# A decoder-block kernel on one core: every engine's order of work rewritten between the first convolution and the last picks

## The reference, cut to what matters

```python
h = _L0_tok_ref(x, positions, ...)                   # [16, 128, 64]
h = h + _L0_attn_ref(_layernorm(h), ...)             # linear recurrence over 128 steps
h = h + _L0_ffn_ref(_layernorm(h), ...)              # 8 experts, one chosen per token

# _L0_tok_ref
h = gelu(conv1d(onehot, w1, b1, 3)); h = gelu(conv1d(h, w2, b2, 2))
ctx = sigmoid(conv1d(h, w3, b3, 1))
amps = emb[ids] * ctx
for s in range(4):
    z = (position - center) / width_s
    basis_total += exp(-0.5 * z * z) * cos(phase + 2 * pi * z) * amp_scale * scale_weights[s] ** 2
field = einsum('bsp,bsd->bpd', basis_total, amps)

# _L0_attn_ref: complex poles, states h_t = A h_{t-1} + u_t, y = Re(C h)
# _L0_ffn_ref
H = gelu(xf @ W1 + b1)                               # 64 -> 256
probs = softmax(H @ Wg + bg)                         # 8 experts
out = probs[chosen] * (H @ Wd[chosen] + bd[chosen])
```

## Time and profile before

| | us |
|---|---|
| Time, median of 3 runs | 111.67 |
| Lowest and highest run | 111.58, 112.59 |
| The profiled execution's own time | 111.52 |
| Its span in the profile | 109.6 |
| TensorE busy (723 instructions) | 100.5 (92%) |
| VectorE busy (230) | 90.0 (82%) |
| ScalarE busy (126) | 70.8 (65%) |
| GpSimd busy (101) | 51.0 (47%) |
| TensorE's granted clock | 1.00 |

### The profile page before, as it was taken

One profiled execution on the slowest core, in us unless ns is written; L12 is line 12 of the kernel. 1 busy time (PEld: TensorE's weight loads), 2 busy tenths in 40 slices (PEclk: granted clock), 3 DMA queues, 4 the chain that ended last, 5 costly groups with the idle time before them and its releaser, 6 DMA issues.

```text
span 109.6 us, 2018 instructions
## 1 busy us (share of the span) xinstructions
PE 100.5 (92%) x723; PEld 64.3 (59%) x723; DVE 90.0 (82%) x230; ACT 70.8 (65%) x126; POOL 51.0 (47%) x101
## 2 busy tenths in 40 slices
PE   5979999999999978869899999999999799999970
PEld 2356785364434576347567477876696476776640
DVE  0359999999999949999999599678999956199892
ACT  4604599999999999999869438454758513551000
POOL 7798998899980007205509426256005000000670
PEclk9999999999999999999999999999999999999999
DMA  3999700000000100000000000000000000000044
GB/s 91 269 233 408 283 0 0 3 0 0 6 0 4 5 0 0 0 0 6 0 0 0 0 6 0 0 0 0 0 0 9 0 0 0 0 0 0 0 96 96
DMA packets 4313, 4.15 MB, mean 38 GB/s; under 512 B 3280, under 2 KB 3536, under 8 KB 4176
## 3 DMA queue, kind: packets, MB, share of 16 engines
q1 hardware_dynamic: 4160, 3.92, 12.5%
q10 hardware_dynamic: 144, 0.12, 0.4%
HBM read 3.50 MB, written 0.52 MB: 37 GB/s over the span
## 4 chain that ended last, share of the span: by engine, by line
PE 42%; ACT 38%; DVE 8%; DMA 4%; issue 4%; POOL 2%; ACTq 0%; DVEq 0%
PE pair L1080 14%; ACT wave L476 8%; PE bank L1042 7%; ACT bell L466 7%; ACT bell L470 5%; ACT L425 5%; DMA ids<-x 4%; DVE pair L819 3%; PE hid_pair L1053 3%; PE pair L951 3%; ACT angle L514 3%; PE pair L921 2%; ACT h L460 2%; PE hid_pair L1063 2%; ACT dist L455 2%
## 5 line engine op out<-in xcount | busy, mean ns | idle before, releaser
L379 POOL TENSOR_SCALAR var_eps<-mean_var 128x4 f32<-128x4 f32 x8 | 3.7, 458 | 33.0 <-DVE mean_var L747 33.0
L819 DVE COPY_PREDICATED pair<-later,pair 128x256 f32<-128x256 int32 (+3 forms) x30 | 12.3, 409 | 5.3 <-PE pair L1080 4.6
L921 PE MATMUL pair<-warm 128*128 128x512 bf16 x53 | 13.3, 380 | 0.0
L732 DVE SCALAR_TENSOR_TENSOR bell<-bell,scale_w,wave 128x512 f32<-128x512 f32 x16 | 10.8, 743 | 0.0
L1080 PE MATMUL pair<-wd_high,H_high 128*128 128x512 f32 x32 | 10.8, 418 | 0.0
L921 PE MATMUL hid_pair<-warm 128*128 128x512 bf16 x30 | 9.0, 455 | 1.3 <-POOL warm L298 1.3
L1080 PE MATMUL pair<-wd_low,H_high 128*128 128x512 f32 x32 | 10.0, 394 | 0.0
L395 POOL TENSOR_TENSOR angle<-picked,prob 128x256 f32<-128x256 f32 x3 | 1.8, 613 | 17.2 <-DVE prob L843 17.2
L521 ACT ACTIVATE bell<-hid_pair,sm 128x512 f32<-128x512 f32 x8 | 5.0, 680 | 7.2 <-PE hid_pair L1053 7.2
L675 DVE TENSOR_TENSOR wave<-dist,inv_width 128x2048 f32<-128x2048 f32 x4 | 9.3, 2356 | 0.0
L965 PE MATMUL pair<-h,w_sb 128*64 128x512 f32 x40 | 9.1, 597 | 0.0
(11 more groups left out here) (166 smaller groups left out, 226.1 us busy)
## 6 DMA issues: line engine op xcount, KB each, us to landing
ids<-x SPq DMA_DIRECT2D x2, 512.0 KB, 5.7
posb<-positions SPq DMA_DIRECT2D x1, 768.0 KB, 8.1
wd_sb<-wd SPq DMA_DIRECT2D x1, 512.0 KB, 9.1
out<-angle SPq DMA_DIRECT2D x3, 128.0 KB, 2.0
st_sb<-state SPq DMA_DIRECT2D x1, 328.0 KB, 8.3
w_sb<-w SPq DMA_DIRECT2D x1, 256.0 KB, 6.6
posb<-positions SPq DMA_DIRECT2D x1, 256.0 KB, 6.6
w_sb<-w SPq DMA_DIRECT2D x1, 160.0 KB, 8.0
```

Of the source, the lines that this page charges most:

```text
L732: ins = dve.scalar_tensor_tensor(out=bell[:, g, part], in0=bell[:, g, part], scalar=scale_w[:, s:s + 1], in1=wave[:, g, part], op0=ALU.mul ...
L819: return dve.copy_predicated(held[:, :, 0:n, 0, 0:D], repeat(later[:, g, 2 * h + rows.start:2 * h + rows.stop, first:first + n], 3, D), he ...
L921: pe.matmul(bank[free], warm[:, 0:P], warm[:, :], start=True, stop=True)
```

## The change

No step is added or dropped except warming matmuls; the steps keep their sizes. It does this:

- conv 1 goes group by group, both parts of the weights at once, and four warming matmuls ahead of it go.
- `turns` is parted into `phases` (four instructions) and `wrap` (the mask), called apart; `product` takes a range of scales, and products 0, 2 and 3 are issued in pieces with other steps between.
- For group 0 of each layer norm VectorE adds epsilon, not GpSimd.
- On ScalarE the scaling of `decay` goes behind field_out(1), the copy of `gate_w` ahead of conv2_out(0); conv2_out(1) ahead of upright_out(0), transposed_out(0, 0) ahead of square(3), normalise(0, 1) ahead of cosine(3), and the gelu table ahead of transposed_out(0, 1).
- GpSimd's powers come in the order (0,0) (0,1) (1,0) (0,2) (1,1) (0,3) (1,2) (1,3).
- TensorE's order from context(1) to the last experts is new; `keep_warm` can wait for a semaphore first.
- At the end logits_back(3, 4) stands behind experts_high(3, 0), and VectorE does both first picks of group 3 ahead of the probability.

The order of GpSimd's finish(g) and of SyncE's issues is unchanged.

```diff
--- before.py
+++ after.py
@@ -376,11 +376,11 @@
             def inv_std(n, g):
                 pool.wait_ge(s_mv[n], g + 1)
-                link(pool.tensor_scalar(var_eps[:, n, g, :], mean_var[:, n, g, :, 1], EPS, None, ALU.add))
                 if g == 0:
                     pool.tensor_tensor(rstd[:, n, g, :], var_eps[:, n, g, :], minus_half[:, 0:GB],
                                        ALU.pow).then_inc(s_rstd[n], 1)
                 else:
+                    link(pool.tensor_scalar(var_eps[:, n, g, :], mean_var[:, n, g, :, 1], EPS, None, ALU.add))
                     pool.tensor_scalar(negated[:, n, g, :], mean_var[:, n, g, :, 0], -1.0, None, ALU.mult)
                     link(pool.tensor_tensor(rstd[:, n, g, :], var_eps[:, n, g, :], minus_half[:, 0:GB], ALU.pow))
                     pool.tensor_tensor(offset[:, n, g, :], negated[:, n, g, :], rstd[:, n, g, :],
@@ -400,10 +400,10 @@
             inv_std(0, 0)
             inv_std(0, 1)
+            inv_std(1, 0)
             inv_std(0, 2)
-            inv_std(1, 0)
+            inv_std(1, 1)
             inv_std(0, 3)
-            inv_std(1, 1)
             inv_std(1, 2)
             inv_std(1, 3)
             for g in range(G - 1):
@@ -548,11 +548,11 @@
             conv1_out(3)
             square(1)
             act.wait_ge(s_poles, 1)
-            act.wait_ge(s_ones_decay, 1)
-            act.activation(decay[:, :, :], decay[:, :, :], ACT.Copy, scale=spar[:, 2:3]).then_inc(s_decay, 1)
             act.wait_ge(ld["state"], 16)
             act.activation(C_part[:, 0, :], C_im, ACT.Copy, scale=spar[:, 4:5]).then_inc(s_C_part, 1)
             act.activation(C_part[:, 1, :], C_im, ACT.Copy, scale=spar[:, 3:4]).then_inc(s_C_part, 1)
+            act.wait_ge(s_gate_pad, 1)
+            act.copy(gate_w[:, :, 0:NE], Wg).then_inc(s_gate_w, 1)
             conv2_out(0)
             load_exp()
             gaussian(0)
@@ -560,49 +560,49 @@
             gaussian(1)
             context_out(0)
             cosine(0)
+            square(2)
             cosine(1)
-            square(2)
             cosine(2)
             field_out(0)
             load_gelu()
+            conv2_out(1)
             upright_out(0)
-            conv2_out(1)
             load_exp()
+            gaussian(2)
             field_out(1)
+            act.wait_ge(s_ones_decay, 1)
+            act.activation(decay[:, :, :], decay[:, :, :], ACT.Copy, scale=spar[:, 2:3]).then_inc(s_decay, 1)
             taps_out(1)
-            gaussian(2)
             upright_out(1)
+            transposed_out(0, 0)
+            square(3)
+            gaussian(3)
             context_out(1)
-            square(3)
-            transposed_out(0, 0)
-            gaussian(3)
             load_sin()
+            normalise(0, 1)
             cosine(3)
-            act.wait_ge(s_gate_pad, 1)
-            act.copy(gate_w[:, :, 0:NE], Wg).then_inc(s_gate_w, 1)
+            load_gelu()
+            transposed_out(0, 1)
             field_out(2)
-            normalise(0, 1)
-            upright_out(2)
-            transposed_out(0, 1)
-            load_gelu()
             act.wait_ge(ld["wd"], 16)
             act.copy(wd_high[:, :, :], wd_sb[:, :, :]).then_inc(s_wd_high, 1)
-            normalise(0, 2)
+            transposed_out(1, 0)
+            upright_out(2)
             field_out(3)
-            transposed_out(0, 2)
-            upright_out(3)
-            transposed_out(1, 0)
             hidden(0)
             round_hidden(0)
-            normalise(0, 3)
+            upright_out(3)
             gate_out(0)
-            transposed_out(0, 3)
+            normalise(0, 2)
+            transposed_out(0, 2)
             normalise(1, 1)
             transposed_out(1, 1)
+            normalise(0, 3)
+            hidden(1)
+            transposed_out(0, 3)
+            round_hidden(1)
+            gate_out(1)
             normalise(1, 2)
-            hidden(1)
-            gate_out(1)
-            round_hidden(1)
             transposed_out(1, 2)
             hidden(2)
             round_hidden(2)
@@ -678,7 +678,7 @@
                     repeat(inv_width[:, g, :, :].rearrange("p s b -> p (s b)"), 2, P),
                     ALU.mult).then_inc(s_z[g], 1)
-            def turns(g):
+            def phases(g):
                 dve.wait_ge(s_z[g], 1)
                 for b in range(GB):
@@ -687,6 +687,9 @@
                         wave[:, g, :].rearrange("p (s b t) -> p s b t", s=NS, b=GB)[:, :, b, :],
                         phase[:, g * GB + b:g * GB + b + 1], TURN, ALU.add, ALU.mult)
                 link(ins)
+
+            def wrap(g):
+
                 dve.tensor_scalar(angle[:, g, :], angle[:, g, :], TURN_MASK, None,
                                   ALU.bitwise_and).then_inc(s_angle[g], 1)
@@ -722,17 +725,19 @@
                 dve.tensor_tensor(amps[:, cols, :], bank[4 + q].rearrange("p (b d) -> p b d", d=D),
                                   repeat(gain[:, cols], 2, D), ALU.mult).then_inc(s_amps, 1)
-            def product(g):
-
-                dve.wait_ge(s_bell[g], 1)
-                for s in range(NS):
+            def product(g, scales):
+
+                if scales.start == 0:
+                    dve.wait_ge(s_bell[g], 1)
+                for s in scales:
                     if s % 2 == 0:
                         dve.wait_ge(s_cos[g], s // 2 + 1)
                     part = slice(s * T, (s + 1) * T)
                     ins = dve.scalar_tensor_tensor(out=bell[:, g, part], in0=bell[:, g, part],
                                                    scalar=scale_w[:, s:s + 1], in1=wave[:, g, part],
                                                    op0=ALU.mult, op1=ALU.mult)
-                ins.then_inc(s_prod[g], 1)
+                if scales.stop == NS:
+                    ins.then_inc(s_prod[g], 1)
             def moments(n, g):
@@ -745,6 +750,9 @@
                 link(ins)
                 for b in range(GB):
                     ins = dve.bn_aggr(mean_var[:, n, g, b, :], stats[:, n, g, b, :])
+                if g == 0:
+                    link(ins)
+                    ins = dve.tensor_scalar(var_eps[:, n, g, :], mean_var[:, n, g, :, 1], EPS, None, ALU.add)
                 ins.then_inc(s_mv[n], 1)
             def normalise(n, g):
@@ -851,72 +859,85 @@
             z(0)
             z(1)
-            turns(0)
-            turns(1)
+            phases(0)
+            wrap(0)
+            phases(1)
+            wrap(1)
             z(2)
-            turns(2)
+            phases(2)
+            wrap(2)
+            input_gain()
+            product(0, range(0, 2))
             gates(0)
-            product(0)
-            product(1)
+            product(0, range(2, NS))
             z(3)
+            product(1, range(NS))
+            phases(3)
             moments(0, 0)
-            turns(3)
+            wrap(3)
             normalise(0, 0)
-            gates(1)
-            product(2)
-            input_gain()
+            product(2, range(0, 2))
             moments(0, 1)
             driven(0)
             scan(0)
             turn_back(0)
-            product(3)
-            moments(0, 2)
+            product(2, range(2, 3))
+            gates(1)
+            product(2, range(3, NS))
             residual(0)
             moments(1, 0)
+            product(3, range(0, 3))
+            normalise(1, 0)
             driven(1)
+            product(3, range(3, NS))
             scan(1)
-            normalise(1, 0)
             turn_back(1)
+            moments(0, 2)
+            weights_rest()
+            residual(1)
+            moments(1, 1)
+            split_hidden(0)
             moments(0, 3)
+            route(0)
             driven(2)
-            weights_rest()
             scan(2)
             turn_back(2)
-            residual(1)
-            moments(1, 1)
+            pick(0, 0)
             residual(2)
             moments(1, 2)
-            split_hidden(0)
-            route(0)
             driven(3)
+            split_hidden(1)
             scan(3)
             turn_back(3)
-            pick(0, 0)
-            split_hidden(1)
+            pick(0, 1)
             residual(3)
             moments(1, 3)
             route(1)
-            pick(0, 1)
+            pick(1, 0)
             split_hidden(2)
-            pick(1, 0)
+            pick(1, 1)
             route(2)
-            pick(1, 1)
             pick(2, 0)
             split_hidden(3)
+            pick(2, 1)
             route(3)
             softmax_in()
-            pick(2, 1)
+            for jj in range(2):
+                pick_last(0, jj)
             probability()
             dve.wait_ge(s_prob, 1)
-            for h in range(2):
-                for jj in range(2):
-                    pick_last(h, jj)
-                    finish_last(h, jj)
+            for jj in range(2):
+                finish_last(0, jj)
+            for jj in range(2):
+                pick_last(1, jj)
+                finish_last(1, jj)
```

(80 more changed lines are left out.)

## The result

| | before | changed |
|---|---|---|
| Time, median | 112.12 us (4 runs) | 116.19 us (4 runs) |
| Lowest and highest | 111.58, 112.59 | 115.12, 116.31 |
| Profiled execution: time, span | 111.52, 109.6 | 115.12, 113.3 |

What follows compares the result with a forecast made beforehand. Bound by ScalarE to about 57 us, then TensorE. TensorE would end 0.9 us earlier, but later `prob`, GpSimd's finish and SyncE's issues make it +2.55 us: 111.52 becomes 114.07, stated as 114.0, range 112.2 to 115.2.

Steps and rivals of the forecast that it cites:

- The tail: After TensorE's last logits: logits at 100.8, `prob` at 104.8 instead of 102.15, GpSimd ends 109.1, last issue 110.05 instead of 107.50.
- The front up to the first power: Start to GpSimd's first power: ScalarE 1.1 us early, cosines at 29.1, power from 42.25 to 44.2.
- Rival B: GpSimd's power of group 0 runs without being held, ending at 43.3 instead of 44.2; time 113.1, chance 0.13.
- The giving back on ScalarE: Group 0's 2.9 us lead ends: 10.6 us of ScalarE work, gelu table included, puts transposed_out(0, 1) at 56.4, before 56.15.
- outputs(0) starts at 50.8: TensorE, group 0: driven(0) at 47.4 instead of 50.26, a lead of 2.9 us, lets outputs(0) start at 50.8.
- s_drive and s_modes stand where TensorE has only outputs(0) to wait for: Warming matmuls ahead of outputs(0): their new semaphore waits cost nothing.
- loses four warming matmuls (1.0 us): TensorE ahead of conv 1: removing them saves 1.0 us; group 0 closes after 8 of 32 matmuls, at 11.6.
- The long stretch: TensorE from field(3) at 60.0: 44.8 us of work plus 0.3 for waits, ending at 105.1 against 106.03.
- already out of the 44.8: TensorE's long stretch: some of the old 0.6 us of gaps were already excluded, so new waits add only 0.3 us.
- Rival C: TensorE's unbroken stretch hides weight loads and runs shorter; 43.0 instead of 44.8 us gives 112.2; chance 0.20.
- rival D: More waits in TensorE's new queue, from slower powers and later group 2 inputs: another 1.2 us, 115.2; chance 0.09.

Runs made afterwards that it cites:

- gates_only: Changed kernel with gates(1) straight behind turn_back(0), ahead of the two last pieces of product(2); ratio to the kernel before 1.0277.
- tail_undone: Changed kernel with the old tail on both engines: logits_back(3, 4) early, probability ahead of group 3's picks; ratio to the kernel before 1.0096, median 113.02 us.
- prob_first: Changed kernel with the probability straight after softmax_in, ahead of both first picks of group 3, logits_back(3, 4) still late; ratio to the kernel before 1.0216.
- logits_early: Changed kernel with only logits_back(3, 4) moved ahead of experts_low(2, 1), VectorE's order kept; ratio to the kernel before 1.0403.
- tail_early_fill: tail_undone with 17 instead of 14 warming matmuls in the first run of them; ratio to the kernel before 1.0087.
- tail_warms: Changed kernel with the old tail and the four warming matmuls around embeddings(0) put back; ratio to the kernel before 1.0203.
- warms_back: Changed kernel with only the four warming matmuls around embeddings(0) put back; ratio to the kernel before 1.0424.
- tail_warms_gates: tail_warms with gates(1) straight behind turn_back(0), ahead of the two last pieces of product(2); ratio to the kernel before 1.0055.

## Why the prediction was wrong

The direction, the tail and more than half of the size were right; the time was 2.2 us too low, and the range missed it by 1.0. Of the 2.2 us, 1.05 are in the profiled execution, and 1.07 are what the median lies above it. That execution alone, at 115.12, lies inside the range.

- **The tail**, the largest term, held: logits to `prob` 4.0 us (100.8 to 104.8 forecast, 101.94 to 105.94 measured), GpSimd 4.19 forecast and 4.15 measured from its first start to its last end, SyncE's last issue 1.0 later. Undone, it gave 3.2 us back; put alone into the kernel before, it took 3.4 to 4.0.
- **The front up to the first power** held within 0.4 us: cosines at 29.49 (29.1), transposed_out(0, 0) at 45.92 (45.75), driven(0) at 47.67 (47.4). The power ended at 44.36. By the Trainium skill's shared port pair (SBUF — State Buffer, Who interferes with whom) it had to wait for the mask, which ended at 43.46, and 1.02 more is 44.48; the trace agrees within 0.12 us. Rival B, 43.3, was out.
- **The giving back on ScalarE** held: transposed_out(0, 1) at 56.54 (56.4).
- **The step that failed in the queues** is "outputs(0) starts at 50.8", with "s_drive and s_modes stand where TensorE has only outputs(0) to wait for". Outputs(0) also waits for the amplitudes of groups 2 and 3, because it writes the bank that holds their embeddings. The wait stands in the code of the kernel before and cost nothing there, since gates(1) was done at 46.4. The change moves gates(1) behind a piece of product(2), to 52.4. Outputs(0) came at 52.52. I took gates(1) out of the way of driven(0) in VectorE's list and did not ask who else waits for it.
- What followed from it was not one cost but two. In the queues: residual(0) 1.7 us late, the product of group 3 0.9 us late (60.34 against 59.4) and field(3) 0.5 us late, worth up to 0.5 us at the end (gates_only: 112.8 to 113.1 against 113.3). And in the clock: 1.6 us of idle time on TensorE, which I had no term or rival for. In the profiled execution the clock stayed up. With the old tail and the early matmuls back, the same gap cost 1.0 to 2.6 us, and filling it brought that back in 11 of 12 executions.
- **The step that failed in the clock** put it at nothing: the sum has TensorE at the upper level throughout, and no term, bound or rival for anything else. That is the larger miss, since it put the median outside the range. The warming matmuls taken out ahead of conv 1 ("loses four warming matmuls (1.0 us)") were booked as a gain alone. The early start did shorten the front, conv 1 at 9.81 (forecast 9.7) instead of 10.36, but it came with a lower clock from 8.6 to 12 us in part of the executions, 0.9 us (tail_undone). The changed kernel's own median lies 1.07 us over its profile. Its other executions left no trace, so which of the two falls they had is not shown. For the early one: prob_first, tail_undone and gates_only have the changed kernel's order up to 50 us, and of their three profiles two had the early fall, 0.9 and 1.4 us above the best spans of their kernels, and none the late one. Against it: logits_early had both falls, and the late one alone can cost as much (tail_early_fill, profiled at 111.4 against spans of 110.1 to 111.0 without it).
- **The long stretch**: 44.8 + 0.3 were forecast and 45.66 came, from field(3) at 60.49 to 106.15. The work was right, 44.87 us busy (the row below), and so were the two waits, 0.51 us ahead of turn(1, 1) and 0.27 ahead of turn(1, 2), where 0.4 and 0.1 to 0.4 were forecast. The slip is in the sum: it counted only 0.3 for them, because gaps of the old stretch were "already out of the 44.8". They were all out of it, since 47.8 is busy time. Rival C, the stretch running faster unbroken, had nothing for it, and rival D was real but smaller than priced. Busy time by stretch of the changed kernel (columns as in the earlier trace rows, after the length of the stretch):

```profile
60.50:106.15 45.65, 44.87 (x312) 32.44 (x312) 36.19 (x114) 21.22 (x49) 10.94 (x21) 1.00 0.00 1
```

In sum: 0.49 us at field(3), which goes with outputs(0), and 0.56 from the stretch, both in the profile, make the 1.05 between the 114.07 worked out and the 115.12 measured for the profiled execution. The rest, to the median, goes with a lower granted clock (0.963 to 0.970 against 0.987), at a place that stays open.

## What to carry to other kernels

Before a step is moved in an in-order queue, list everyone who waits for its semaphore, not only the consumer it was written for: a wait that has always been met long ago costs nothing until its producer is moved. When the last work hangs on one small result (here a softmax denominator that holds back another engine's four microseconds and the issues behind it), put that result first, ahead of work that is larger but only its own. And a gap on TensorE can be priced twice, once as waiting and once by what runs after it at the lower clock; filler matmuls are part of the schedule, and taking them out needs a look at the granted clock in more than one execution.

## What the runs showed of the hardware

A gap of 1.59 us on TensorE, with busy stretches on both sides, was followed by the lower clock in tail_warms, 0.5 us after it ended (granted clock 0.79 from 50 to 56 us and 0.64 from 56 to 62), while in the profile of the changed kernel the same gap passed without it. Over all profiles that have this gap ahead of outputs(0), 1.58 or 1.59 us, the clock fell behind it in four (tail_warms, warms_back, tail_early_fill, logits_early) and not in three (changed, prob_first, tail_undone). With a gap of 0.92 us none of four profiles showed it, though 3 of 12 executions of tail_warms_gates still had a granted clock of 0.978 to 0.985, and six matmuls of zeros in the gap were worth 1.1 us. The early fall shows in three of the five profiles without the four warming matmuls and with 14 at the start, in none of the seven with the four, and in neither of the two with 17 at the start.

One and the same program runs at two or three heights, 1 to 3 us apart. The kernel before does so too, but seldom: 8 of 63 executions had a granted clock of 0.985 or less and spans of 111.1 to 113.9. How often it happens differs with the order of the instructions: in all six of tail_warms, in one of twelve with the gap filled. None of this was in my forecast.
